# One clip per tile of h moved from VectorE to GpSimd, in the last stage of a gated cross-attention and FFN block

## The reference, cut to what matters

```python
QMAX = 127.0
def _act_fake_quant(x, clip_factor):
    scale = sigmoid(clip_factor) * max(abs(x)) / QMAX
    return clip(round(x / scale), -QMAX - 1.0, QMAX) * scale

x = x + tanh(g_xattn[0]) * cross_attention(layernorm(x), ctx)
xq = _act_fake_quant(layernorm(x), clip_x[0])
gate = einsum("bsh,ih->bsi", xq, weight_fake_quant(w_gate))      # i = 704
up   = einsum("bsh,ih->bsi", xq, weight_fake_quant(w_up))
h    = _act_fake_quant(silu(gate) * up, clip_down[0])            # one scale for all of h
x = x + tanh(g_ffn[0]) * einsum("bsi,hi->bsh", h, weight_fake_quant(w_down))
```

## Time and profile before

| | |
|---|---|
| time, median of 3 runs | 274.58 us (274.26 to 275.72) |
| the profiled execution's own time | 274.51 us |
| its span, first to last instruction | 272.7 us |
| busy in the span: TensorE, VectorE, ScalarE, GpSimd | 81%, 81%, 61%, 51% |
| the stage of the down products (first L802 to the end) | 249.02 to 272.7 us |
| its instructions: L802, L1157, L1163 | 16 each |
| its instructions: L1179, L597, L600, L1192 | 8, 5, 2, 2 |

### The profile page before, as it was taken

The page is one execution under the profiler, slowest core; times in us unless marked ns, Lnnn a source line. Parts: engine busy times, 40 slices in busy tenths (PEclk is TensorE's granted clock), DMA queues, the critical chain, the costliest instruction groups (busy, mean ns, idle before and its releaser), DMA issues.

```text
span 272.7 us, 5672 instructions
## 1 busy us (share of the span) xinstructions
PE 221.3 (81%) x1656; PEld 144.1 (53%) x1660; DVE 222.1 (81%) x455; ACT 166.2 (61%) x300; POOL 138.9 (51%) x221
## 2 busy tenths in 40 slices
PE   0698999989969999999999898979741788962982
PEld 0587888768635565655566565635420333321751
DVE  3369999979976988888998989888558279997995
ACT  1325576476756567666676667677733478864960
POOL 3366657544431425276566748387485154340274
PEclk9979999999989999999999999999995599995698
DMA  6939859998344333444433332000002300000098
GB/s 230 252 94 343 262 159 273 290 283 219 100 135 129 104 94 93 110 117 118 117 107 106 81 103 77 1 3 1 2 2 77 118 1 1 0 2 1 1 127 180
DMA packets 34184, 30.78 MB, mean 113 GB/s; under 512 B 5232, under 2 KB 27760, under 8 KB 34160
## 3 DMA queue, kind: packets, MB, share of 16 engines
q1 hardware_dynamic: 29776, 27.74, 35.9%
q0 software_dynamic: 1360, 1.31, 4.1%
q10 hardware_dynamic: 3024, 1.44, 1.9%
HBM read 20.65 MB, written 9.70 MB: 111 GB/s over the span
## 4 chain that ended last, share of the span: by engine, by line
PE 43%; DVE 21%; issue 13%; ACT 10%; POOL 7%; DMA 3%; DVEq 1%; ACTq 1%; SPq 0%; POOLq 0%
PE bank_o L1368 10%; PE bank_a L1351 9%; PE bank_b L1338 5%; PE bank_m L1376 4%; ACT big L701 3%; PE bank_b L1483 3%; PE bank_a L1259 3%; DVE arena L835 2%; DVE stats L825 2%; ACT arena L701 2%; DVE arena L1157 2%; PE bank_a L1483 2%; DVE h_max L1117 2%; ACT wgu_rows L802 1%; DVE big L1126 1%
## 5 line engine op out<-in xcount | busy, mean ns | idle before, releaser
L845 DVE TENSOR_REDUCE neg_max<-bank_b 128x2 f32<-128x512 f32 x128 | 80.6, 675 | 5.2 <-PE bank_b L1248 3.0
L1351 PE MATMUL bank_a<-big 98*128 98x256 bf16 x256 | 49.8, 277 | 9.9 <-ACT big L701 4.0
L701 ACT ACTIVATE arena<-bank_a 128x512 f32<-128x512 f32 x64 | 36.2, 605 | 19.0 <-PE bank_a L1351 19.0
L701 ACT ACTIVATE big<-bank_a 128x512 f32<-128x512 f32 x64 | 35.5, 595 | 18.1 <-PE bank_a L1351 17.8
L1338 PE MATMUL bank_b<-big 96*128 96x256 bf16 x224 | 43.3, 275 | 0.2 <-issue 0.2
L1351 PEld LDWEIGHTS bank_a<-big 98*128 98x128 bf16 x256 | 18.5, 98 | 33.7 <-ACT big L701 12.3
L1259 PE MATMUL bank_a<-arena,w_t 128*128 128x256 f32 x128 | 31.9, 398 | 0.5 <-DVE resid L856 0.5
L1259 PEld LDWEIGHTS bank_a<-arena,w_t 128*128 128x128 f32 x128 | 24.4, 199 | 4.2 <-DVE resid L856 1.0
L495 POOL CAST max_parts<-max_f 8x256 bf16<-8x256 f32 x16 | 6.2, 388 | 39.5 <-issue 37.0
L1338 PEld LDWEIGHTS bank_b<-big 96*128 96x128 bf16 x224 | 21.3, 99 | 4.9 <-DVE neg_max L845 1.1
L458 POOL TENSOR_TENSOR arena<-resid,arena 128x512 bf16<-128x512 f32 x16 | 18.4, 1164 | 10.7 <-ACT arena L641 10.7
(11 more groups left out here) (161 smaller groups left out, 438.3 us busy)
## 6 DMA issues: line engine op xcount, KB each, us to landing
qk_parts<-arena SPq DMA_DIRECT2D x8, 768.0 KB, 4.6
big<-qk_parts SPq DMA_DIRECT2D x32, 192.0 KB, 3.1
big<-qk_parts SPq DMA_DIRECT2D x32, 128.0 KB, 3.0
x_rows<-in_x SPq DMA_DIRECT2D x8, 256.0 KB, 5.2
big<-qk_parts SPq DMA_DIRECT2D x32, 64.0 KB, 3.1
big<-in_ctx SPq DMA_DIRECT2D x7, 256.0 KB, 4.0
out<-x_rows SPq DMA_DIRECT2D x7, 256.0 KB, 2.5
out<-v_all POOLq DMA_DIRECT2D x5, 256.0 KB, 4.8
```

The lines of the kernel that those rows point to most:

```text
L701: act.activation(probabilities(h), bank_a[:, h % 2].rearrange("p (c s) -> p c s", c=QC), ACT.Exp, scale=SCALE).then_inc(exp_done, 1)
L845: dve.tensor_reduce(neg_max[:, p, :, h], bank.rearrange("p (c s) -> p c s", c=QC), axis=AX.X, op=ALU.max, negate=True).then_inc(max_done, 1)
L1351: done = mm(to, k_st[0:KM, p, h, k * P:(k + 1) * P], q_st[0:KM, p, h], start=True, stop=not masked)
```

## The change

`clip_tile` moves from VectorE's program to GpSimd's. It is still one instruction per tile, with the two immediates 127 and -128, in place on `hq`, and it still raises `hq_ready`. VectorE's `round_tile` gets a second operation (the minimum with 127) in the same instruction, so each VectorE iteration is now two rounds and a `scale_down`. In GpSimd's program the two clips of sequence b come first, then from b = 3 on the accumulating DMA of sequence b - 3; the two additions of sequences 5 and 6 follow behind the last clips. GpSimd's wait for `x2_stored` now stands ahead of the clips.

```diff
+            def clip_tile(i):
+                t = slice(i * P, (i + 1) * P)
+                pool.wait_ge(y_free, i + CT + 1)
+                pool.tensor_scalar(hq[:, :, t], hq[:, :, t], QMAX, -QMAX - 1, ALU.min, ALU.max).then_inc(hq_ready, 1)
+
+            def add_x(b):
+                pool.wait_ge(y_scaled, b + 5)
+                if b < ONTO:
+                    pool.dma_start(out_dram[:, tiles(b)], v_all[:, tiles(b)], accum_op=ALU.add).then_inc(summed, 16)
+                else:
+                    pool.tensor_tensor(x_rows[:, tiles(b)], x_rows[:, tiles(b)], v_all[:, tiles(b)], ALU.add
+                                       ).then_inc(row_sum, 1)
+
             pool.wait_ge(x2_stored, 16 * ONTO)
-            for b in range(ONTO):
-                pool.wait_ge(y_scaled, b + 5)
-                pool.dma_start(...accum_op=ALU.add).then_inc(summed, 16)
-            for b in range(ONTO, B - 1):
-                pool.wait_ge(y_scaled, b + 5)
-                pool.tensor_tensor(...).then_inc(row_sum, 1)
+            for b in range(B):
+                for c in range(QC):
+                    clip_tile(b * QC + c)
+                if b >= 3:
+                    add_x(b - 3)
+            add_x(B - 3)
+            add_x(B - 2)
...
                 def round_tile(i):
                     dve.wait_ge(y_rounded, i + 1)
-                    dve.tensor_scalar(hq[:, :, i * P:(i + 1) * P], h_round[:, i % CT], -MAGIC, None, ALU.add
+                    dve.tensor_scalar(hq[:, :, i * P:(i + 1) * P], h_round[:, i % CT], -MAGIC, QMAX, ALU.add, ALU.min
                                       ).then_inc(y_free, 1)
-                def clip_tile(i):
-                    t = slice(i * P, (i + 1) * P)
-                    dve.wait_ge(y_free, i + CT + 1)
-                    dve.tensor_scalar(hq[:, :, t], hq[:, :, t], QMAX, -QMAX - 1, ALU.min, ALU.max
-                                      ).then_inc(hq_ready, 1)
-
-                i = b * QC
-                round_tile(i)
-                if b == 0:
-                    clip_tile(i)
-                round_tile(i + 1)
-                if b:
-                    clip_tile(i)
-                clip_tile(i + 1)
+                for i in range(b * QC, b * QC + QC):
+                    round_tile(i)
```

More of the change, by code:

```diff
@@ L593, in _ @@
                         over_scale(3)
-            pool.wait_ge(x2_stored, 16 * ONTO)
-            for b in range(ONTO):
-                pool.wait_ge(y_scaled, b + 5)
-                pool.dma_start(out_dram[:, tiles(b)], v_all[:, tiles(b)], accum_op=ALU.add).then_inc(summed, 16)
-            for b in range(ONTO, B - 1):
-                pool.wait_ge(y_scaled, b + 5)
-                pool.tensor_tensor(x_rows[:, tiles(b)], x_rows[:, tiles(b)], v_all[:, tiles(b)], ALU.add
-                                   ).then_inc(row_sum, 1)
+            def clip_tile(i):
[9 more added lines that the diff above has]
+                                       ).then_inc(row_sum, 1)
+            pool.wait_ge(x2_stored, 16 * ONTO)
+            for b in range(B):
[5 more added lines that the diff above has]
+            add_x(B - 2)
         @block.scalar
```

## The result

| kernel | time, median | ratio to before (95%) | span | stage |
|---|---|---|---|---|
| before | 274.49 us (274.26 to 275.72, 4 runs) | | 272.7 | 23.68 |
| changed | 284.13 us (281.96 to 285.99, 4 runs) | 1.0339 (1.0254 to 1.0424) | 281.5 | 31.21 |

The change makes the kernel 3.4% slower; 284.3 was forecast. "Stage" is from ScalarE's first instruction of the last stage (L802 before, L817 now) to the end of the span. The changed stage is 31.21 - 23.68 = 7.5 us longer; 1.3 us of the span's 8.8 are not the change's.

A forecast was written before the change was run, and what follows sets the result against it. GpSimd becomes the bound, clips and rounds excluding each other: from 250.65, six tiles at 1.30, sequence 3 at 2.19, four periods of 3.67, a tail to 279.28, stores to 282.5; +9.8 us gives 284.3 us, range 279 to 298.

The forecast's parts named there:

- The price of a clip, 0.89 us: One 768-element clip on GpSimd: fixed 0.193 us plus 0.694 us at 0.904 ns per element, from L578 and L446.
- rival 2: Dearer clip on GpSimd: bfloat16 minimum and maximum at the two-input rate, 1.74 us, time 297.9 us; chance 0.19.
- The issue, 1.48 us, taken in full: Each of five accumulating DMA issues occupies GpSimd for all its 1.48 us, in one queue with the clips.
- rival 3: Issues don't delay GpSimd's next clip and rounds slip past clips, so all follows ScalarE: 273.1 us; chance 0.05.
- the variant of rival 1: Rounds and clips exclude each other, but issues don't occupy GpSimd: 16 x 1.30 us of clips, time 279.0 us.
- An issue does not stop a round: VectorE's rounds beside GpSimd's five DMA issues keep their mean of 0.556 us.
- The meeting, 0.41 us per round: VectorE round and GpSimd clip don't overlap: 0.41 us charged, making 0.89 + 0.41 = 1.30 us per tile where they alternate.
- rival 1: No meeting or a cheaper one: rounds and clips pass each other, GpSimd alone sets the pace, 280.0 us; chance 0.14.
- The schedule: GpSimd in the last stage: clips from 250.65, last clip over at 275.32, additions at 279.28, stores at 282.5 us.
- rival 4: Both rounds meet the clips in each sequence: 4.08 instead of 3.67 us, time 286.3 us; inside the forecast's 0.62.
- What was covered: Last tile's matmuls, `scale_down` and VectorE additions, 3.0 us behind the last clip, hide under GpSimd's 3.96 us tail, even at half clock.
- ScalarE should wait for L1157: Sign of the forecast: ScalarE, held by its ring, waits for VectorE's round in the last stage; no size given.

The follow-up runs named there:

- run 1: Changed kernel without its five accumulating DMAs on GpSimd, all waits kept: stage 25.28 us, time 279.61 us, ratio 1.0114.
- run 2: Changed kernel with GpSimd's clip on 2 elements in place of 768: stage 23.67 us, time 276.52 us, ratio 1.0033.
- run 5: Changed kernel with clips of 384 instead of 768 elements: stage 27.09 us, time 278.25 us, ratio 1.0117.
- run 3: Changed kernel with one extra two-operation VectorE round after each round of sequences 3 to 7, ten in all: stage 32.39 us, time 284.42 us, ratio 1.0316.
- run 10: Kernel before with only the four clips of sequences 1 and 2 moved to GpSimd: stage 25.05 us, time 277.04 us, ratio 1.0055.
- run 4: Changed kernel with ten extra VectorE reductions of 400 float32 elements, about as long as a round: stage 31.02 us, time 284.05 us, ratio 1.0282.
- the repetition: The changed kernel unaltered, once more: stage 31.13 us, time 283.45 us, ratio 1.0316.
- run 6: Kernel before with only the minimum with 127 added to the round, both clips left on VectorE: stage 23.73 us, time 276.69 us, ratio 1.0023.
- run 9: Changed kernel with the five accumulating issues behind the last clip instead of between clips: stage 32.65 us, time 285.27 us, ratio 1.036.
- run 7: Kernel before with ScalarE writing int16 and one VectorE instruction per tile for clip and conversion to bfloat16: stage 20.90 us, time 273.31 us, ratio 0.9919.

## Why the prediction was right, step by step

**The bound.** Right: GpSimd sets the pace, and VectorE's relief is worth nothing. Runs 1, 2 and 5 each took work off GpSimd, and the stage became 5.9, 7.5 and 4.1 us shorter.

**The price of a clip, 0.89 us.** It is 0.82; the slope was 0.833 instead of 0.904 ns per element. Bfloat16 and minimum/maximum cost nothing extra, so rival 2 is out.

**The issue, 1.48 us, taken in full.** Taking it in full was right (run 1), which excludes rival 3 and the variant of rival 1. The size was mis-sized: 1.53 for the first and 1.21 to 1.23 for the other four. The 1.48 of before had a wait for VectorE in it (run 3; in run 10 the same issues took 1.20). "An issue does not stop a round" holds for the rounds and was only a part of the question: VectorE's instructions hold up an issue, and in run 10 issues seem to have held up VectorE's clips.

**The meeting, 0.41 us per round.** The mechanism is shown by runs 3 and 4, so rival 1 is out. The size was too large: where clip and round alternate, a tile takes 1.09 and not 1.30. Of that 0.08 is a gap between instructions and 0.20 the meeting (a clip of 1.02 instead of 0.82). By the rule of the Trainium skill ("SBUF — State Buffer", section "Who interferes with whom"), read as excluding whole instructions, a tile would be 0.82 + 0.56 = 1.37. The trace agrees that they exclude each other, and differs by 0.28 us per tile in how much of each counts.

**The schedule.** In microseconds from the start of the stage, forecast and measured: end of the eighth clip 11.6 and 10.7; last clip 26.3 and 24.0; GpSimd's additions over 30.3 and 27.8; end 33.5 and 31.2. Up to the end of the eighth clip 0.9 us of the forecast were too many, from there to the last clip 1.4, and behind it nothing. The four periods with an issue were to be 3.67 each, 14.68; they were 3.75, 3.38, 3.08 and 3.08, 13.29. The prediction has one round meet the clips in each of the four. The trace has two in each of the first two (rival 4's case) and none in the last two, which follows from the prediction's own limit: VectorE is two sequences ahead, so its last rounds ran beside the clips of sequence 5 and were over 5.8 us before the last clip ended. The number of meetings, four, was right all the same, and by luck. The sizes were not: the issues made 0.7 us less than forecast, the clips alone 0.6 less and the four meetings 1.0 less (0.64 instead of 1.64: the eight clips' 7.52 us less eight times 0.82 and four gaps of 0.08), against 0.9 us of gaps between instructions that the sum had at nothing. In all that is the 2.3 us by which the stage was forecast too long (+9.8 forecast, +7.5 measured).

**Why the number fits better than its sum.** 284.3 against 284.13 us is partly luck: the stage was 2.3 us shorter than forecast, and in the profiled execution it began 1.3 us later. That the latter is chance is shown by the repetition, which began at 248.47. The profiled execution took 283.32 us; the other 0.8 are what the median of the four runs lies above it.

**What was covered.** TensorE's half clock came back, covered as forecast. VectorE's last additions were held up to the end of GpSimd's, as allowed for. "ScalarE should wait for L1157" was wrong: its sixteen instructions still took 14.80 us. At 1.09 us per tile the lag stays inside the ring of four until ScalarE is done. Only behind the extra instructions of runs 3 and 4 did it wait, 1.7 and 0.5 us.

## What to carry to other kernels

Before moving work to an idle engine, add up that engine's period with all that already stands in its queue, DMA issues included, and ask whether the move's two sides exclude each other: here 0.36 us of VectorE became 0.82 on GpSimd, behind 1.21 of issues, and the clips slowed the rounds that they were meant to relieve, even where GpSimd had nothing else to do. Count the waits in both directions: VectorE's rounds lengthened the issues, and in run 10 VectorE's own clips became longer where the issues had become shorter. Look at how far the next engine lies below the bound (here ScalarE, 0.11 us per tile), since that caps the gain. The way out was to need fewer instructions, by leaving the rounding to the producer's output type.

## What the runs showed of the hardware that was not expected

**The start of the stage goes along with TensorE's granted clock.** With the same program in front of it, the stage began between 248.5 and 252.8 us in thirteen profiles. Window 75 to 205 us of the repetition and of run 6 (the number behind POOL's is the granted clock):

```profile
75.00:205.00 130.00, 115.06 (x1105) 69.41 (x1103) 109.53 (x228) 85.78 (x173) 71.69 (x115) 0.99 0.30 81
```

```profile
75.00:205.00 130.00, 117.37 (x1109) 70.61 (x1108) 109.08 (x224) 86.30 (x175) 70.92 (x114) 0.96 0.30 81
```

The four profiles with 0.95 or 0.96 there began the stage at 252.3 to 252.8, the nine with 0.97 or 0.99 at 248.5 to 250.3. The window doesn't tell all: the changed kernel's two profiles both have 0.99 in it and began the stage at 250.29 and 248.47, and between 16 and 60 us they have 0.96 and 1.00. What makes the clock differ isn't shown, nor is it shown to be the only cause. It is a difference of 2 to 4 us with the same program in front, as large as many effects that one wants to see, and a reason to compare stages instead of ends.

**A VectorE addition with two inputs in SBUF waits for GpSimd's issues too.** In run 9 the first 128x256 addition, 0.42 us where free, started at 271.39 beside the row of issues and took 2.54:

```profile
269.63 6.39 POOL L604 DMA_DIRECT2D out<-v_all  x5
271.39 2.54 DVE L1194 TENSOR_TENSOR x_rows<-x_rows,v_all 128x256 f32<-128x256 f32 x1
```

Up to 273.61 the trace has nothing but issues on GpSimd; whether they or GpSimd's addition, whose span is shown from there on, held it for the rest, to 273.93, is open. VectorE's instructions are not held alike: rounds beside an issue take 0.55 to 0.63 us instead of 0.56 (run 3), the clips of run 10 took up to 0.52 instead of 0.35 beside issues of 1.2, and the int16 clips of run 7 up to 0.75 instead of 0.36.
